# Dividing the causal softmax on the probabilities instead of on the head outputs

## The reference, cut to what matters

```python
def attention(h, wq, wk, wv, wo):
    ...
    scores = jnp.einsum('bhqd,bhkd->bhqk', q, k) / jnp.sqrt(jnp.float32(D))
    causal = jnp.tril(jnp.ones((s, s), bool))
    scores = jnp.where(causal, scores, jnp.finfo(scores.dtype).min)
    attn = jax.nn.softmax(scores, axis=-1)
    out = jnp.einsum('bhqk,bhkd->bhqd', attn, v)
    out = out.transpose(0, 2, 1, 3).reshape(b, s, NH * D)
    return out @ wo
```

## Time and profile before

| | us |
|---|---|
| median of 3 runs | 1047.88 (1045.89 to 1048.29) |
| profiled execution | 1048.07 |
| its span in the profile | 1046.5 |
| start to about 55 us: first modulation and projections | 55 |
| units 0 to 63, windowed | 354 |
| units 64 to 127, causal (409 to 797 us) | 388 |
| routing, experts, output | 249 |

### The profile page before, as it was taken

The page is one execution under the profiler, slowest core; times in us unless marked ns, Lnnn a source line. Parts: engine busy times, 40 slices in busy tenths (PEclk is TensorE's granted clock), DMA queues, the critical chain, the costliest instruction groups (busy, mean ns, idle before and its releaser), DMA issues.

```text
span 1046.5 us, 22627 instructions
## 1 busy us (share of the span) xinstructions
PE 958.1 (92%) x6862; PEld 899.4 (86%) x6862; DVE 747.4 (71%) x2180; ACT 745.2 (71%) x2058; POOL 469.9 (45%) x566
## 2 busy tenths in 40 slices
PE   5679999999899999999999999999997599999991
PEld 3469999999889999989999999999887499999991
DVE  6657887778788667877777777677764766666646
ACT  3258787888788888888888788877885355555541
POOL 4347667868656533433453232232223852222243
PEclk8889999999899999999999999999998799999996
DMA  8779798897466776465547464454303375555313
GB/s 184 179 180 281 216 230 253 235 231 190 112 172 159 205 198 169 125 159 134 132 141 156 122 171 122 112 141 133 81 2 113 124 252 157 171 164 163 104 59 118
DMA packets 146056, 166.15 MB, mean 159 GB/s; under 512 B 79194, under 2 KB 100714, under 8 KB 140816
## 3 DMA queue, kind: packets, MB, share of 16 engines
q1 hardware_dynamic: 129440, 143.58, 52.7%
q0 software_dynamic: 3712, 11.16, 3.3%
q10 hardware_dynamic: 12784, 9.97, 3.1%
HBM read 105.88 MB, written 58.79 MB: 157 GB/s over the span
## 4 chain that ended last, share of the span: by engine, by line
PE 64%; DVE 12%; ACT 8%; issue 8%; DMA 3%; POOL 3%; SPq 1%; ACTq 0%; DVEq 0%; POOLq 0%
PE psO L1131 16%; PE psS L1098 11%; PE psX L1108 10%; PE psY L1147 8%; PE psP L1030 7%; ACT wgt_hi L1364 3%; DVE gated L2112 2%; PE psO L1114 2%; PE psP L1060 2%; PE psP L1043 2%; POOL xg L937 2%; DVE pbuf L1788 2%; DVE pTl L1798 1%; ACT relu_s L1670 1%; PE psS L1281 1%
## 5 line engine op out<-in xcount | busy, mean ns | idle before, releaser
L1407 ACT ACTIVATE pbuf<-pbuf,nmax 128x257 f32<-128x257 f32 (+5 forms) x512 | 264.3, 518 | 41.1 <-DVE nmax L1788 39.7
L1788 DVE CUSTOM_DVE_ANT_0 pbuf<-psS,mcau 128x256 f32<-128x256 f32 (+3 forms) x512 | 221.4, 435 | 79.5 <-PE psS L1098 69.6
L1098 PE MATMUL psS<-kT,qE 128*128 128x256 f32 (+3 forms) x1024 | 236.5, 316 | 14.2 <-DVE nmax L1788 13.2
L1798 DVE TENSOR_TENSOR pTl<-psX,pTh 128x512 fp32r<-128x512 f32 x272 | 187.0, 688 | 73.4 <-ACT pTh L1364 72.7
L1364 ACT ACTIVATE pTh<-psX 128x512 fp32r<-128x512 f32 x272 | 160.5, 590 | 59.1 <-PE psO L1131 41.0
L1131 PE MATMUL psO<-pTh,vpad 128*128 128x256 f32 x1088 | 187.0, 294 | 3.3 <-DVE oS L1804 2.6
L827 POOL TENSOR_TENSOR ol<-oS,oh 128x256 fp32r<-128x256 f32 x128 | 94.8, 741 | 200.3 <-ACT oh L1364 195.7
L1098 PEld LDWEIGHTS psS<-kT,qE 128*128 128x128 f32 x1024 | 160.9, 192 | 24.1 <-DVE nmax L1788 18.1
L1108 PE MATMUL psX<-idn,pbuf 128*128 128x128 f32 x1088 | 162.5, 274 | 5.3 <-DVE pTl L1798 5.2
L1131 PEld LDWEIGHTS psO<-pTh,vpad 128*128 128x128 f32 x1088 | 150.3, 190 | 10.8 <-DVE oS L1804 5.6
L1108 PEld LDWEIGHTS psX<-idn,pbuf 128*128 128x128 f32 x1088 | 126.7, 141 | 11.8 <-DVE pTl L1798 5.7
(11 more groups left out here) (294 smaller groups left out, 2304.9 us busy)
## 6 DMA issues: line engine op xcount, KB each, us to landing
qE<-qd SPq DMA_DIRECT2D x128, 256.0 KB, 6.1
qd<-st SPq DMA_DIRECT2D x24, 1024.0 KB, 4.7
mrawV<-in_w_moe SPq DMA_DIRECT2D x32, 384.0 KB, 3.6
mrawB<-in_w_moe SPq DMA_DIRECT2D x32, 384.0 KB, 3.3
kT<-kd SPq DMA_DIRECT2D x64, 128.0 KB, 4.5
kT<-kd SPq DMA_DIRECT2D x32, 256.0 KB, 4.4
qd<-tmp SPq DMA_DIRECT2D x8, 1024.0 KB, 4.2
kd<-st SPq DMA_DIRECT2D x5, 1024.0 KB, 4.8
```

What stands on the lines that cost most here:

```text
L1098: last = mm(psS[j % 2][:, 0:n], qE[:, g % 2, j, t * P:(t + 1) * P], kT[:, g % 2, c, k0:k0 + n], start=(c == 0), stop=(c == 1))
L1407: nc.scalar.activation(pj, src, ACT.Exp, bias=nmax[:, u % 4, j:j + 1], scale=-1.0, accum_out=sums[:, u % 4, j:j + 1]).then_inc(a_exp, 1)
L1788: V.tensor_tensor_reduce(dst, psS[j % 2][:, 0:n], mcau[:, SEQ - n:], -SCALE, 3e38, ALU.add, ALU.min, nmax[:, u % 4, j:j + 1]).then_inc(v_m ...
L1798: V.tensor_tensor(pTl[:, kt % 2, :], psX[kt % 2][:, :], pTh[:, kt % 2, :], ALU.subtract).then_inc(v_pl, 1)
```

## The change

For the causal units the probabilities are divided before they are turned. `denominator(u)` moves one step ahead, to right behind the first `mask_max` of step u+1, and three new `divide(u)` follow it: VectorE multiplies head 0 with its reciprocal, GpSimd heads 1 and 2, ScalarE head 3 (behind its second exponential). `turn_probs(u, 0)` waits for all three. `spread`, `turn_scale`, `scale_of`, `scale_out` and `out_low` are left out for these units; ScalarE's `out_hi` now copies the value product from PSUM, one step earlier, and VectorE's new `out_lo` takes the rest from PSUM and frees psO. On TensorE, `out_project` moves one unit earlier and to behind scores 2, value product 0 of u-2 to ahead of the projection, and each later value product to right behind the turn of its own key tile.

```diff
 # GpSimd
+            def divide(u):
+                pool.wait_ge(v_rden, u + 1)
+                apart(pool)
+                for j in (1, 2):
+                    G.tensor_scalar(probs(u, j), probs(u, j), rden[:, u % 4, j:j + 1], None, ALU.mult).then_inc(g_norm, 1)
...
-                if 0 <= u - 4 < NU:
+                if 0 <= u - 4 < W:
                     out_low(u - 4)
+                if W <= u - 1 < NU:
+                    divide(u - 1)
...
-                if 0 <= u - 1 < NU:
+                if 0 <= u - 1 < W:
                     spread(u - 1)
 # TensorE
                 if k == 0:
-                    pe.wait_ge(a_exp, QM * (u + 1))
+                    if windowed(u):
+                        pe.wait_ge(a_exp, QM * (u + 1))
+                    else:
+                        pe.wait_ge(v_norm, u - W + 1)
+                        pe.wait_ge(g_norm, 2 * (u - W + 1))
+                        pe.wait_ge(a_norm, u - W + 1)
...
                 if now:
                     scores(u, 2)
-                if u - 3 < NU:
+                if u - 3 < W:
                     turn_scale(u - 3)
+                if u < W + 5:
+                    out_project(u - 5)
+                if W + 4 <= u < NU + 4:
+                    out_project(u - 4)
                 if nk > 1:
                     turn_probs(u - 2, 1)
                 if now:
                     scores(u, 3)
+                if nk > 1:
+                    values(u - 2, 0)
                 if now and ahead(u):
                     project(ahead(u))
                 if nk > 2:
                     turn_probs(u - 2, 2)
-                if nk > 1:
-                    values(u - 2, 0)
-                if nk > 2:
                     values(u - 2, 1)
                 if nk > 3:
                     turn_probs(u - 2, 3)
-                out_project(u - 5)
-                if nk > 3:
                     values(u - 2, 2)
 # ScalarE
+            def divide(u):
+                act.wait_ge(v_rden, u + 1)
+                last = probs(u, QM - 1)
+                nc.scalar.activation(last, last, ACT.Copy, scale=rden[:, u % 4, QM - 1:QM]).then_inc(a_norm, 1)
...
                     exp_head(u, 0)
-                if u - 3 < NU:
+                if u - 4 < W:
+                    out_hi(u - 4)
+                if u - 3 < W:
                     scale_of(u - 3)
+                elif u - 3 < NU:
+                    out_hi(u - 3)
                 if now:
                     exp_head(u, 1)
+                if W <= u - 1 < NU:
+                    divide(u - 1)
 # VectorE
+            def divide(u):
+                dve.wait_ge(v_rden, u + 1)
+                V.tensor_scalar(probs(u, 0), probs(u, 0), rden[:, u % 4, 0:1], None, ALU.mult).then_inc(v_norm, 1)
+
+            def out_lo(u):
+                dve.wait_ge(a_oh, u + 1)
+                V.tensor_tensor(ol[:, u % 2, :], psO[:, 0:2 * P], oh[:, u % 2, :], ALU.subtract).then_inc(v_ol, 1)
...
                     mask_max(u, 0)
+                if W <= u - 1 < NU:
+                    denominator(u - 1)
+                    divide(u - 1)
+                if now:
                     mask_max(u, 1)
...
-                if u - 3 < NU:
+                if u - 3 < W:
                     scale_out(u - 3)
-                if u - 2 < NU:
-                    denominator(u - 2)
+                elif u - 3 < NU:
+                    out_lo(u - 3)
```

More of the change, by code:

```diff
@@ L65, in windowed @@
     return u < 2 * SEGU
+W = 2 * SEGU
 def keys(u):
@@ L402, in build @@
         v_rden = sem("v_rden")
+        v_norm = sem("v_norm")
+        v_ol = sem("v_ol")
+        a_norm = sem("a_norm")
+        g_norm = sem("g_norm")
         v_pl = sem("v_pl")
@@ L1119, in values @@
                 if k == 0:
-                    wait(pe, v_os, u)
+                    wait(pe, v_os, min(u, W))
+                    wait(pe, v_ol, u - W)
                     if u % QUAD < TB:
@@ L1137, in out_project @@
                 seg, t, g = u // SEGU, u % TB, u // TB
-                pe.wait_ge(g_ol, u + 1)
+                if windowed(u):
+                    pe.wait_ge(g_ol, u + 1)
+                else:
+                    pe.wait_ge(v_ol, u - W + 1)
                 if t == 0:
@@ L1419, in scale_of @@
                 copy(rS[:, u % 2, :], psO[:, 2 * P:4 * P]).then_inc(a_rx, 1)
+            def divide(u):
+                act.wait_ge(v_rden, u + 1)
+                last = probs(u, QM - 1)
+                nc.scalar.activation(last, last, ACT.Copy, scale=rden[:, u % 4, QM - 1:QM]).then_inc(a_norm, 1)
             def out_hi(u):
-                act.wait_ge(v_os, u + 1)
+                if windowed(u):
+                    act.wait_ge(v_os, u + 1)
+                else:
+                    act.wait_ge(s_PV, KT[u + 1])
                 wait(act, s_Y, u - 1)
-                copy(oh[:, u % 2, :], oS[:, u % 2, :]).then_inc(a_oh, 1)
+                copy(oh[:, u % 2, :], oS[:, u % 2, :] if windowed(u) else psO[:, 0:2 * P]).then_inc(a_oh, 1)
             squared = [0]
```

8 lines of the change are left out of this document (5 added, 3 removed).

## The result

The changed kernel takes 1070.05 us (median of 4 runs, 1066.54 to 1072.59); the kernel before, in the same comparison, 1047.81 (4 runs). The ratio is 1.0216, with a 95% interval of 1.0200 to 1.0231: the change makes the kernel 2.2% slower. The profiled execution is the fastest of the four, 1066.54 us with a span of 1065.0. A difference of 0.3% can be told from none here.

A forecast was written before the change was run, and what follows sets the result against it. TensorE was taken to set the pace of the causal units, with 7.1 us idle. New waits of 45.7 us, less 7.1 idle and 15.3 gains, gave +23.3 on 1048.07: 1071.4 us, range 1056 to 1087.

The forecast's parts named there:

- step 1: Causal step making a one-key unit's scores and multiplying a three-key unit; new waits forecast at 14.0 us.
- step 2: Causal step making a two-key unit's scores, multiplying a four-key unit; waits forecast: 11.0 us, plus 11.2 behind a projection.
- step 4: Causal step making a four-key unit's scores, multiplying a two-key unit; waits forecast behind a projection: 11 x 0.86 = 9.5 us.
- Value product 2 in step 2: Four-key unit's third product: 2.13 us from turn 2, with 1.43 of TensorE work between; 16 x 0.69 = 11.0 us.
- the term for the weights: In the time from VectorE's start to the value matmul: 0.12 us added because the weights come first.
- The late `take`: Projection at a step's end: `take` ends 1.5 us into the next step, delaying masks; terms 14.0, 9.5 and 11.2 us.
- step 3: Causal step making a three-key unit's scores, multiplying a one-key unit; wait below 0.35 us a step, left out.
- the 7.1 us of idle time of before: TensorE's idle time in the old causal stage, taken off because the 45.7 us of new waits sit at its places.
- TensorE's idle share: Sign in the changed profile: TensorE idle some 10% of a causal stage of about 411 us.
- The turned reciprocals: Two matmuls of `turn_scale` leave TensorE's queue in each step: 64 x 0.20 = 12.8 us gained; last unit another 2.5.
- Rival A: TensorE still sets the pace, queue 15.3 us shorter: 1032.8 us, first masks at 0.5 to 0.8 us; chance 0.20.
- Rival C: VectorE's division stands still until GpSimd's weight subtraction ends, in 31 of 64 steps: 20 us, 1091; chance 0.09.

The follow-up runs named there:

- experiment 1: Changed kernel with projection, value product 0 and output projection back in TensorE's old order, division kept: 1043.65 us, ratio to before 0.9969.
- experiment 2: Changed kernel with only the projection put back ahead of value product 0, output projection still early: 1050.23 us, ratio 1.0032.
- experiment 4: Kernel before, with turned reciprocals and no division, in the changed kernel's TensorE order: 1077.34 us, ratio 1.0294.
- experiment 6: Changed kernel with VectorE dividing one column of its head instead of all: 1066.99 us.
- experiment 3: Changed kernel with only the output projection put back late, between the last turn and value product 2: 1070.22 us, ratio 1.0220.
- experiment 9: As experiment 1, but output projection early, ahead of turn 1, in step 4 and in step 1 without a projection: 1039.83 us, ratio 0.9926.
- experiment 8: As experiment 1, with VectorE's `out_lo` ahead of the third mask instead of behind it: 1044.30 us, ratio 0.9980.
- Experiment 7: Changed kernel with GpSimd and ScalarE dividing one column of their three heads instead of all: 1065.15 us.
- experiment 11: Projection before turn 2, output projection early or ending step 3 (1050.00 us); then the projection's copy and `take` before the third turn's copy and rest: 1047.94 us.
- experiment 12: As experiment 11, with the output projection of step 2 behind the last turn as before the change: 1040.40 us, ratio 0.9938.

## Why the prediction was right

The forecast was 1071.4 us, the median is 1070.05, and the mechanism is in the main the forecast's. Experiments 1 and 2 show that with the division kept the loss goes when TensorE's order is put back, and experiment 4 shows that the order alone makes a loss in steps 1 and 2. In step 4 it takes both: the order alone leaves it at 6.27, and experiment 6 finds VectorE's division in its loss. By the forecast's steps:

- **Value product 2 in step 2.** 2.13 us from turn 2 were forecast, 2.01 measured. The 0.12 between them is the term for the weights, which no row shows: the three hand-overs took 0.63, 0.63 and 0.75, and the product started with its weights. The price is right: experiments 1 and 2 differ only in the place of the output projection, and step 2 is 0.70 longer where it is early, 11.2 us for the forecast's 11.0.
- **The late `take`.** First mask of step 1 forecast at 1.5, measured 1.43; `out_lo` at 3.4, measured 3.35; value product 0 at 4.0 (step 1), 4.12 (step 2), 5.11 (step 4), measured 3.87, 3.88, 4.92, each behind a projection. Right to within 0.25, and the forecast is always a little late.
- **The sums.** Net of the turned reciprocals the terms make, for 16 groups, step 1 +10.8, step 2 +19.0, step 3 -3.2, step 4 +6.3, together +32.9; less the 7.1 us of idle time of before that is 25.8. The table, x 16, gives +8.0, +14.7, -3.5, +6.2, together +25.4. So the sum is right, and the 7.1 us had to come off. Whether they are the old idle time, or make up for waits counted too long, these lengths do not tell.
- **TensorE's idle share.** Some 10% were forecast, the profile shows 25 of 410 us, 6%. In the row of value product 2 it shows 0.27 us of idle time, where the turn before it started 0.87 us earlier and a turn costs 0.35: half of the wait of 0.52 lies under the modelled end of the matmul before it. Other waits were not measured so.
- **What the count of the waits missed.** It takes a wait as the chain's length from the step's beginning less TensorE's queue. Experiment 3 shows a ring instead: shortening the queue ahead of value product 0 gives nothing, and only to break the ring (experiment 2, the projection ahead of value product 0) gives the time back. In the ring value product 2's 11.0 us cannot be had on their own: with the output projection moved back for it, step 2 fell by 0.40, 6 us, and steps 3 and 4 took them back.
- **The order and the division apart.** The sum has 45.7 - 7.1 = 38.6 us of loss by the order and 15.3 of gain by the division. Experiment 4 finds 30 and 7: both some 8 us short, and the two cancel. The count itself gives a reason: where value product 0 waits, two matmuls less ahead of it only lengthen the wait, by 0.20 in each of the 41 steps counted, 8.2 us. But experiment 4 waits in part at other places, so how much of the agreement is luck stays open.
- **The turned reciprocals.** 0.20 a step were forecast. The shortest steps of a kind in experiment 9 against before are 6.41 for 6.62 (step 1, with a projection), 6.97 for 7.11 (2, without), 3.42 for 3.49 (3, without) and 6.26 for 6.48 (4, with): 0.64 a group, 10 us for 12.8. The last unit gave 2.95 for 2.5. Right, but under the old order the group is only 0.11 shorter. What the forecast priced at nothing there, VectorE's reciprocals and division ahead of the masks, is the likely cause in step 4, where `out_lo` is late (experiment 1): with `out_lo` ahead of a mask (experiment 8) step 4 gains 0.30, but other steps lose it. That it takes back all of the rest is not shown. In the changed kernel VectorE's division lay inside the counted chain.
- **Rival A** (TensorE's pace, 1032.8) did not come: the first masks are at 1.3 to 1.5 behind a projection. No kernel's median here reaches it. The best steps of all kernels that do the whole work, 6.39 + 7.67 + 4.04 + 5.92 = 24.02, would give 16 x 0.70 + 2.95 = 14.2 us; whether one order can have all four is open.
- **Rival C** (VectorE's division behind GpSimd) happened once in 64, ahead of the 410 us from which the table counts:

```profile
405.50 1.29 POOL L798 TENSOR_TENSOR wkvl<-wkvraw,wkvh 128x512 fp32r<-128x512 f32 x1
...
405.89 1.12 DVE L1845 TENSOR_SCALAR pbuf<-pbuf,rden 128x384 f32<-128x384 f32 x1
```

GpSimd's weight subtraction began 0.39 us ahead and lasted until 406.79; VectorE's division of 384 columns took 1.12 instead of 0.42 and ended 0.22 behind it. (34 steps have such a subtraction in the trace, not 31.) The Trainium skill, page "SBUF — State Buffer", section "Who interferes with whom", has it that such instructions shut each other out whole and the first wins; this row agrees. In the other direction GpSimd's first division pays beside VectorE's:

```profile
632.59 3.33 POOL L860 TENSOR_SCALAR pbuf<-pbuf,rden 128x512 f32<-128x512 f32 x2 [4.06 <-DVE rden L1830]
...
634.36 1.56 POOL L860 TENSOR_SCALAR pbuf<-pbuf,rden 128x512 f32<-128x512 f32 x1
```

The first one of 512 columns takes 3.33 - 1.56 = 1.77 us, the second 1.56. With VectorE's division cut from 0.49 to 0.21 (experiment 6) the first takes 1.57. So the price is 0.2 us, less than the 0.36 that VectorE's division still had to run in its row when GpSimd's began, and less than that rule would give.

GpSimd's divisions were done nearer to their use than forecast. In unit 97 they end at 623.66, 0.48 us ahead of turn 0. In unit 65, at the stage's beginning, turn 0 waited 1.17 us for them (405.64), which the forecast had named as a sign of being wrong. Experiment 7 shows that all this is worth little.

## What to carry to other kernels

When two instructions in one engine's queue are exchanged, ask whether the one that now comes later starts a chain through other engines that ends, in the next round, at the one that comes first. Such a ring kept its length here when work was moved off the queue (experiment 3), and undoing one exchange of neighbours (experiment 2) was worth 20 us.

An instruction that is to fill a hand-over between engines is best placed by the buffer that it gives time to, not by the wait that looks late: moving the late mask (experiment 11) brought 2 us, filling the time until the buffer's copy is used (experiment 12) 7.5 more.

And work taken off the busiest engine is worth its time only if what it becomes elsewhere does not stand ahead of something that this engine waits for: of 15.3 us, 3.6 were left under the old order.

## What was not expected of the hardware

- A multiplication by a column of scalars takes, from 128 to 512 columns, 0.29 to 0.49 us on VectorE, 0.40 to 0.71 on ScalarE and 0.60 to 1.56 on GpSimd (0.5, 0.8 and 2.5 ns a column). Cut to one column it still takes VectorE 0.21.
- TensorE's busy time is no measure of its work: with 128 matmuls fewer and 25 us idle, the stage shows 385 busy us instead of 381.
